# The inverse of the softmax sums: from a reciprocal on VectorE to a power of minus one on GpSimd

## What is computed

```python
gate_logits = (h @ W_a.T).reshape(B, T, H, M, M + 1)
gates = jax.nn.softmax(gate_logits, axis=-1)
a0 = gates[..., 0]
A = gates[..., 1:]
u_t = a0 * v                                  # v = h @ W_v.T
new = einsum('bhij,bhj->bhi', A_t, state) + u_t   # one step per token, in order
```

## Time and profile before

| what | value |
|---|---|
| median of 3 runs | 780.73 us (779.34 to 780.85) |
| profiled execution | 785.26 us, its span 783.5 us |
| VectorE busy | 678.8 us, 87% of the span |
| GpSimd busy | 567.7 us, 72% |
| ScalarE busy | 552.9 us, 71% |
| TensorE busy | 590.8 us, 75% |
| instructions in the trace | 12543 |

### The profile page before, as it was taken

How to read it: one execution, slowest core, us unless ns; L and a number is a source line. 1 busy time by engine, 2 the same in 40 slices (tenths; PEclk the granted TensorE clock), 3 DMA queues, 4 the chain that set the end, 5 groups by cost and what they waited for, 6 DMA issues and landing times.

```text
span 783.5 us, 12543 instructions
## 1 busy us (share of the span) xinstructions
PE 590.8 (75%) x2826; PEld 443.5 (57%) x2826; DVE 678.8 (87%) x2921; ACT 552.9 (71%) x1272; POOL 567.7 (72%) x635
## 2 busy tenths in 40 slices
PE   5785144787968697887879697977879785898886
PEld 3242022565746575665657475765657564688775
DVE  4569999999999999999999989899998999999431
ACT  4764142777786868787777868686877868587775
POOL 2685556687878797887878787887878777756354
PEclk9886565899999999999999989898989999899998
DMA  6365655463736446354637364454538264640000
GB/s 176 97 147 139 136 119 131 105 135 79 169 86 140 112 122 124 77 132 101 143 79 166 88 134 116 106 126 82 129 76 173 72 152 95 140 113 8 14 8 8
DMA packets 162235, 85.35 MB, mean 109 GB/s; under 512 B 77752, under 2 KB 156784, under 8 KB 157936
## 3 DMA queue, kind: packets, MB, share of 16 engines
q1 hardware_dynamic: 162160, 84.55, 46.7%
HBM read 44.66 MB, written 39.85 MB: 108 GB/s over the span
## 4 chain that ended last, share of the span: by engine, by line
DVE 61%; PE 17%; issue 9%; ACT 8%; POOL 2%; DMA 1%; SPq 1%; POOLq 0%; ACTq 0%; DVEq 0%
DVE ps L998 14%; DVE prod L990 13%; DVE ps L1004 8%; DVE act_t L1070 7%; PE ps L1437 7%; DVE nmax L968 6%; DVE zs L975 5%; PE ps L1450 4%; PE ps L1424 3%; DVE rz L981 2%; ACT ex L659 2%; ACT ps L693 1%; ACT up L687 1%; PE ps L1481 1%; ACT L693 1%
## 5 line engine op out<-in xcount | busy, mean ns | idle before, releaser
L1437 PE MATMUL ps<-h2t,wgu 128*128 128x256 f32 x1024 | 259.0, 396 | 24.6 <-ACT up L687 24.6
L1437 PEld LDWEIGHTS ps<-h2t,wgu 128*128 128x128 f32 x1024 | 194.2, 198 | 71.8 <-ACT up L687 29.8
L1424 PE MATMUL ps<-wl,ht 128*128 128x512 f32 (+1 forms) x320 | 167.2, 625 | 71.3 <-ACT lg L670 67.3
L1450 PE MATMUL ps<-wd,act_t 128*128 128x128 f32 x1024 | 146.1, 288 | 61.6 <-DVE act_t L1070 58.5
L1450 PEld LDWEIGHTS ps<-wd,act_t 128*128 128x128 f32 x1024 | 135.3, 199 | 88.6 <-DVE act_t L1070 77.1
L998 DVE TENSOR_REDUCE ps<-prod 128x8 f32<-128x136 f32 x512 | 152.8, 298 | 10.6
L990 DVE TENSOR_TENSOR prod<-gates,ps 128x136 f32<-128x136 f32 x512 | 147.4, 288 | 14.7 <-DMA gates<-gate_dram 6.2
L421 POOL TENSOR_TENSOR lg<-lg,nmax 128x1088 f32<-128x1088 f32 x64 | 130.2, 2038 | 15.0 <-DVE nmax L968 13.1
L745 ACT ACTIVATE weighted<-ps,comb 128x128 f32<-128x128 f32 x256 | 80.1, 364 | 81.5 <-PE ps L1450 78.9
L414 POOL TENSOR_TENSOR ex<-ex,rz 128x1088 f32<-128x1088 f32 x64 | 129.2, 2039 | 9.1 <-DVE rz L981 6.3
L687 ACT ACTIVATE up<-ps,bgu 128x256 f32<-128x256 f32 x256 | 107.4, 474 | 36.7 <-PE ps L1437 36.7
(11 more groups left out here) (122 smaller groups left out, 588.4 us busy)
## 6 DMA issues: line engine op xcount, KB each, us to landing
gate_dram<-ex SPq DMA_DIRECT2D x256, 136.0 KB, 3.2
gates<-gate_dram SPq DMA_DIRECT2D x32, 1088.0 KB, 5.6
yt_tok<-y_dram SPq DMA_DIRECT2D x256, 8.0 KB, 3.5
xg<-in_L_attn_x_dram SPq DMA_DIRECT2D x32, 64.0 KB
y_dram<-ys SPq DMA_DIRECT2D x32, 64.0 KB, 1.7
out_dram<-res_out SPq DMA_DIRECT2D x32, 64.0 KB
wa_rows<-in_L_attn_W_a_dram SPq DMA_DIRECT2D x1, 1088.0 KB, 6.5
dn_rows<-in_L_ffn_down_proj_dram SPq DMA_DIRECT2D x1, 1024.0 KB, 12.3
```

The source lines that it names most:

```text
L1424: nc.tensor.matmul(ps[:, n % 2, 0:w], ht[:, g % RH, j * P:(j + 1) * P], wl[:, k * LC:k * LC + w], start=True, stop=True).then_inc(lg_ps.se ...
L1437: last = nc.tensor.matmul(gu_ps(m, k, which)[:, q * N:(q + 1) * N], wgu[:, k, rows + q * P:rows + (q + 1) * P], h2t[:, m % 2, :], start=Tr ...
L1450: last = nc.tensor.matmul(dn_ps(j), act_t[:, k % 2, q * N + j * P:q * N + (j + 1) * P], wd[:, k, q, :], start=(q == 0), stop=(q == KI - 1))
```

## The change

`row_inverse` is taken from VectorE's stream and written in GpSimd's. It waits there for the same semaphores (the four quarter sums zs_ok, and norm_ok of the chunk before) and raises the same one (rz_ok). The reciprocal of 128x128 elements becomes a tensor_tensor with the operation pow, whose exponent is a new constant column of -1.0 read with a broadcast. It stands behind `gate_value` and ahead of `norm_gates`, for both tiles. `clamp_up(m, 1)`, which stood between `gate_value(e, 0)` and `norm_gates(e, 0, 0)`, goes ahead of `gate_value(e, 0)`. One more memset fills the constant, and two counts of `consts` rise by one.

```diff
--- before.py
+++ after.py
@@ -70,7 +70,7 @@
     QR = HI // NQ
     STEP_INCS = 3
     OTHER_HALF = [(q + NR) % (2 * NR) for q in range(2 * NR)]
-    CONSTS = 7
+    CONSTS = 8
     RX, RH, RN = 6, 5, 3
 
     x_t = x.rearrange("b (n t) d -> n b t d", t=TS)
@@ -116,6 +116,7 @@
         ident = sb("ident", [P, P])
         lower = sb("lower", [P, E, E])
         minus_half = sb("minus_half", [P, 1])
+        minus_one = sb("minus_one", [P, 1])
         eps_mean = sb("eps_mean", [P, 1])
         eps_sum = sb("eps_sum", [P, 1])
 
@@ -379,9 +380,10 @@
             nc.gpsimd.memset(ident[:, :], 0.0).then_inc(consts, 1)
             nc.gpsimd.memset(lower[:, :, :], 1.0).then_inc(consts, 1)
             nc.gpsimd.memset(minus_half[:, :], -0.5).then_inc(consts, 1)
+            nc.gpsimd.memset(minus_one[:, :], -1.0).then_inc(consts, 1)
             nc.gpsimd.memset(eps_mean[:, :], EPS).then_inc(consts, 1)
             nc.gpsimd.memset(eps_sum[:, :], EPS * D).then_inc(consts, 1)
-            pool.wait_ge(consts, 5)
+            pool.wait_ge(consts, 6)
             nc.gpsimd.affine_select(out=ident[:, :], in_=ident[:, :], compare_op=ALU.not_equal, fill=1.0, base=0,
                                     pattern=[[-1, P]], channel_multiplier=1).then_inc(consts, 1)
 
@@ -404,6 +406,13 @@
                 pool.wait_ge(zs_ok.sem, zs_ok.at(e, 4 * (j + 1)))
                 v = ex[:, j, :].rearrange("p (r k) -> p r k", k=M1)
                 nc.gpsimd.tensor_tensor(v[:, :, 0], v[:, :, 0], vv[:, j, :], ALU.mult).then_inc(rv_ok.sem, 1)
+
+            def row_inverse(e, j):
+                pool.wait_ge(zs_ok.sem, zs_ok.at(e, 4 * (j + 1)))
+                if not is_first(e):
+                    pool.wait_ge(norm_ok.sem, norm_ok.at(e - 1, 2 * j + 2))
+                nc.gpsimd.tensor_tensor(rz[:, j, :], zs[:, j, :], minus_one[:, :].broadcast_to([P, HI]), ALU.pow
+                                        ).then_inc(rz_ok.sem, 1)
 
             def norm_gates(e, j, part):
                 if part == 0:
@@ -482,11 +491,11 @@
                     finish(o)
                 if a is not None:
                     first_h(a)
+                if m is not None:
+                    clamp_up(m, 1)
                 if e is not None:
                     gate_value(e, 0)
-                if m is not None:
-                    clamp_up(m, 1)
-                if e is not None:
+                    row_inverse(e, 0)
                     norm_gates(e, 0, 0)
                     norm_gates(e, 0, 1)
                 if m is not None:
@@ -494,6 +503,7 @@
                     clamp_up(m, 2)
                 if e is not None:
                     gate_value(e, 1)
+                    row_inverse(e, 1)
                     norm_gates(e, 1, 0)
                     norm_gates(e, 1, 1)
                 if m is not None:
@@ -974,12 +984,6 @@
                 rows = slice(half * HI // 4, (half + 1) * HI // 4)
                 nc.vector.tensor_reduce(zs[:, j, rows], ex[:, j, :].rearrange("p (r k) -> p r k", k=M1)[:, rows, :], AX_X, ALU.add).then_inc(zs_ok.sem, 1)
 
-            def row_inverse(e, j):
-                dve.wait_ge(zs_ok.sem, zs_ok.at(e, 4 * (j + 1)))
-                if not is_first(e):
-                    dve.wait_ge(norm_ok.sem, norm_ok.at(e - 1, 2 * j + 2))
-                nc.vector.reciprocal(rz[:, j, :], zs[:, j, :]).then_inc(rz_ok.sem, 1)
-
             def scan_products(s, t):
 
                 if t % TS == 0:
@@ -1128,9 +1132,6 @@
                 elif u == 19:
                     if e is not None:
                         row_sum(e, 0, 3)
-                elif u == 20:
-                    if e is not None:
-                        row_inverse(e, 0)
                 elif u == 25:
                     if m is not None:
                         hidden(m, 0)
@@ -1152,9 +1153,6 @@
                 elif u == 36:
                     if m is not None:
                         hidden(m, 1)
-                elif u == 38:
-                    if e is not None:
-                        row_inverse(e, 1)
                 elif u == 39:
                     if g is not None:
                         row_max(g, 0, 1)
```

More of the change, by code:

```diff
@@ L484, in run @@
                     first_h(a)
-                if e is not None:
-                    gate_value(e, 0)
                 if m is not None:
@@ L489, in run @@
                 if e is not None:
+                    gate_value(e, 0)
+                    row_inverse(e, 0)
                     norm_gates(e, 0, 0)
```

## The result

The changed kernel takes 1404.22 us (median of 4 runs, 1404.18 to 1404.59), the kernel before 780.79 us on the same chip. The ratio is 1.7975, with a 95% interval of 1.7918 to 1.8032. The profiled execution takes 1404.59 us, its span is 1402.8 us. The forecast was 1784 us, with a range of 782 to 1834 us. Some executions of the kernels near 780 us take over 1.5% more than the fastest of the same kernel; the ratios and intervals in this document leave these out, the medians don't.

The account below looks back on a forecast made before the run. VectorE was taken to bound the middle of the kernel before, GpSimd the changed one: 785.3 + 1053 for 32 pows - 50 idle time regained = 1788 us, less 4.5 for the median, 1784 us; range 782 to 1834 us.

Parts of the forecast that it names:

- Which case it is: Price of GpSimd's pow: mostly by column (16 us up, 0.46), overlapping columns (1.3 to 16 us, 0.38), no change 0.06, faster 0.10.
- The price of one pow: GpSimd's new 128x128 pow: 519 ns plus 128 columns at 253 ns, 32.9 us; 1.03 us if the cost is per instruction.
- the 506 ns over an addition: GpSimd's traced 128x2 pow, 700 ns, less a 128x2 addition, 194 ns; taken as 253 ns for each column.
- GpSimd's work in full on the path: GpSimd becomes the bound in each of 16 chunks; its work grows by 32 x 32.9 = 1053 us.
- Idle time regained: GpSimd's waits for ScalarE's up values and the weighted results, 94 us: half taken as vanishing, about 50 us.
- VectorE's 22.4 us off the path: VectorE's saving from the removed reciprocals, 22.4 us, no longer counts once GpSimd is the bound.
- The most that can be gained, 22.4 us: VectorE's 32 reciprocals at 0.7 us of path each, if VectorE were the bound all along.
- The rival of a faster kernel: GpSimd's pow costs 506 ns of start-up, 1.03 us in all, and mostly fits its idle time; 772 us, chance 0.10.
- its turning point: About 1.1 us a pow on GpSimd; above it VectorE's wait for xn at second_stats eats all the gain.
- The waits that take the reciprocals' place: On VectorE, waits for clamped up values and xn replace the reciprocals; TensorE's granted clock falls below 0.91 between 37 and 695 us.
- 731 + 32p: Rule for the kernel's time in us when GpSimd's pow takes p us, for p above 2 us.
- The bounds of the prediction's cases: Kernel times by pow price: by column, 16 us and up, 1245 to 1834 us; overlapping, 1.3 to 16 us, 783 to 1245.

Follow-up runs that it names:

- the line of sizes: Kernel before with unread GpSimd pows of 128x4 to 128x128 added at its end; 158.9 ns per column and 383 ns start; timed once, 864.61 us.
- half: Changed kernel with GpSimd's pow on columns 0 to 63 and VectorE's reciprocal on the other 64 of each tile; 1077.44 us.
- 0.8 us: Changed kernel with each pow replaced by two GpSimd multiplications of 128x128 by a constant; 777.32 us, ratio 0.9893 to the kernel before.
- 1.2 us: Changed kernel with each pow replaced by three GpSimd multiplications of 128x128 by a constant; 786.90 us, ratio 1.0037 to the kernel before.

## Why the prediction was right, and where its numbers were off

- *Which case it is.* Right: the price goes by the column, and GpSimd becomes the bound. The measured 20.7 us lies in the stretch that the forecast had (16 us and up), not at its end. The direction came out right because pow was judged to be paid by the column. That the range held 1404.22 us says little, since it ran from no change to 32.9 us a pow; the number itself, 1784, was 380 us too high.
- *The price of one pow.* This is the term that was mis-sized: 32.9 us stated, 20.73 measured. The step that failed is that all of the 506 ns over an addition was put down to two columns. By the line of sizes, two columns cost 2 x 159 = 318 ns and the start 383 ns, which is some 190 ns more than the addition's start (194 - 2 x 2.1 = 190). 32 x (32.9 - 20.73) = 389 us, which is the whole distance between 1788 and the profiled 1404.59 us but for 6. The Trainium skill, page "GPSIMD Engine Reference", section 3.1, gives 2.6 cycles per element for two inputs, where the forecast has about 2.5; by it, 126 more columns would be an estimated 0.27 us instead of 0.26. The trace has 20.73 - 0.70 = 20.03 us for them, which goes with that section's other statement, that the time grows with the operations in the loop's body.
- *GpSimd's work in full on the path.* Right: one for one between half and whole.
- *Idle time regained.* 50 us taken, 41.6 measured, but from other rows. I took half of the waits for up and the weighted results; they fell by 12 us together (94.0 to 82.0). The wait for the statistics, which I thought would stay, fell by 14.4 (27.5 to 13.1). Those for the maxima (13.1 to 3.5), for VectorE's sums (7.3 to 1.6) and for its inverses (6.3 to none) fell by 21.6 together, and the wait of `second_h` for ScalarE rose by 5.5 (7.0 to 12.5). The size was nearly right by luck, since the reasons were mostly wrong: what disappears is waits for VectorE, 36.0 us of them, which had been late and is now early, and only 9.2 us of those for ScalarE.
- *VectorE's 22.4 us off the path.* Right (under 2 us when put back).
- *The most that can be gained, 22.4 us.* Not wrong as a bound, but the kernel without inverses gains 9 us: VectorE ran into `gated_out`, whose wait for TensorE rose from 7.6 to 20.2 us. The earlier trace rows had 17% of the chain on TensorE, and I looked for no rival there.
- *The rival of a faster kernel and its turning point.* Never in play at 20.7 us, but measured: the turn lies between 0.8 and 1.2 us, where 1.1 was stated. That agreement is in part luck. The prediction's own wait, 1.4 + 2p - 0.25 - 1.05 = 2p + 0.1 us in each of 14 chunks, would eat the 22.4 us at p = 0.75 already, and the 1.1 isn't worked out from it. The reason wasn't right either: at 0.8 us the wait for xn is 6.0 us in 8 waits, not 1 us in each of 14 chunks, moving xn forward made the kernel slower, and up to 1.2 us it is `go` that waits.
- *The waits that take the reciprocals' place.* Right in kind: xn (323.6 us) and the clamped up values (255.3 us) on VectorE. TensorE's granted clock also fell as forecast, from a mean of 0.91 in the middle to 0.72 (37 to 1314 us), both between its levels of 1.2 and 2.4 GHz, and its matmuls of the experts went from 396 to 426 ns. What of that is hidden behind GpSimd no run separates; the chain that ended last still has 10% on TensorE. GpSimd was busy for 1166.3 of the 1277 us of that stretch, 91%, where 94% was forecast.
- *731 + 32p.* At 20.73 us it gives 1394, measured 1404.22; at 10.53 us 1068, measured 1077.44. It is 10 us low at both. At the whole pow the parts are known: 8.4 us of idle time that wasn't regained (50 less 41.6) and 4.5 us for a median below the profiled execution, which this time lay only 0.4 us below, make 12.5; of it goes 2.5 us, since GpSimd's busy time grew by 660.9 and not 663.4 us. The bounds of the prediction's cases aren't this rule's: at 16 us it gives 1243 us, where 1245 stands, and at 1.3 us 773, where 783 stands, just above no change. Neither changes the range that was given.

## What to carry to other kernels

A single small size doesn't price an operation: two numbers, a start and a cost per column, need two sizes, and a tiny instruction already in the trace gives only a range. Here the truth lay nearer the end of the cost per column. Before work goes to an engine with idle time, ask how much of that idle time lies between the instruction and the next thing that another engine needs; here 23% idle had room for about 1 us. Where one engine's line was the bound, moving an instruction within it moved the wait to the next reader and won nothing.

## What the runs showed of the hardware that I hadn't expected

- pow on GpSimd is 0.383 us + 0.159 us per column of 128 partitions, the same for exponents -1 and -0.5, for ones and for real data, and with VectorE idle or busy for 4 to 6 us of the 20.7. VectorE's reciprocal of the same 128x128 takes 0.951 us, a 22nd of it.
- A multiplication of 128x128 on GpSimd took 0.40 us where it read and wrote dense tiles and one operand was a broadcast column, 0.45 us with two full operands, and 0.52 us where every 17th element was taken.
- The chain that ended last can hide the engine that bounds: with GpSimd at 88%, the view gives 52% to issue and 3% to the line of the pow; 30 of its pieces of "issue" are the pow.
